# Cross attentions of a two-layer decoder: scores, mask and maximum in pairs of units, and the end of the layer normalisation on GpSimd

## What is computed

```python
def _layernorm(x, axis=-1, eps=1e-05):
    m = jnp.mean(x, axis=axis, keepdims=True)
    v = jnp.var(x, axis=axis, keepdims=True)
    return (x - m) / jnp.sqrt(v + eps)

def _L0_xattn_ref(query, key, value, mask, Wq, bq, Wk, bk, Wv, bv, Wo, bo):
    ...
    scores = jnp.einsum('bhqd,bhkd->bhqk', Q, K) / np.sqrt(D_K)
    m = mask[:, None, :, :]
    scores = jnp.where(m == 0, NEG, scores)
    attn = jax.nn.softmax(scores, axis=-1)
    x = jnp.einsum('bhqk,bhkd->bhqd', attn, V)
    x = x.transpose(0, 2, 1, 3).reshape(b, -1, D_MODEL)
    return x @ Wo.T + bo

x = _layernorm(x + _L0_attn_ref(...))
x = _layernorm(x + _L0_xattn_ref(x, ctx_1024, ctx_1024, mask_BxSxS2_ik0, ...))
x = _layernorm(x + _L0_ffn_ref(...))
x = _layernorm(x + _L1_attn_ref(...))
x = _layernorm(x + _L1_xattn_ref(x, ctx_1024, ctx_1024, mask_Bx1xSxS2_ff0, ...))
x = _layernorm(x + _L1_ffn_ref(...))
```

## Time and profile before

| | |
|---|---|
| median of three runs | 1294.27 us (1292.2 to 1297.17) |
| the profiled execution, its own time | 1291.09 us |
| its span, first to last instruction | 1289.3 us |
| mean granted TensorE clock | 0.924 of full speed |
| busy: PE, DVE, ACT, POOL | 84%, 75%, 55%, 30% of the span |
| first cross attention, first to last score turned | 436.8 to 580.8 us |
| second cross attention, the same | 1055.7 to 1197.2 us |

### The profile page before, as it was taken

The page is one execution under the profiler, slowest core; times in us unless marked ns, Lnnn a source line. Parts: engine busy times, 40 slices in busy tenths (PEclk is TensorE's granted clock), DMA queues, the critical chain, the costliest instruction groups (busy, mean ns, idle before and its releaser), DMA issues. The chain is left out here.

```text
span 1289.3 us, 30260 instructions
## 1 busy us (share of the span) xinstructions
PE 1087.8 (84%) x10763; PEld 881.4 (68%) x10763; DVE 961.6 (75%) x2254; ACT 704.9 (55%) x1459; POOL 388.9 (30%) x538
## 2 busy tenths in 40 slices
PE   4899989999987699986269999389999569999696
PEld 3578878778776577774257777378787447777485
DVE  7587877878875488884938883569998538888497
ACT  2454444444443355552637775368788525655484
POOL 5122222222220355551130000423331225555232
PEclk9899999999999799995559999699999879999799
DMA  6000000100000500005245431300000000000011
GB/s 257 5 10 2 10 12 2 71 3 2 2 2 2 187 23 22 11 9 227 107 135 172 171 108 49 120 17 26 24 9 9 0 24 23 11 21 9 34 50 50
DMA packets 34072, 65.35 MB, mean 51 GB/s; under 512 B 7590, under 2 KB 23334, under 8 KB 30886
## 3 DMA queue, kind: packets, MB, share of 16 engines
q1 hardware_dynamic: 32422, 59.62, 13.2%
q0 software_dynamic: 1536, 4.20, 1.0%
HBM read 43.03 MB, written 12.39 MB: 43 GB/s over the span
## 5 line engine op out<-in xcount | busy, mean ns | idle before, releaser
L953 POOL TENSOR_TENSOR ca_z<-ca_z,ca_top 128x308 f32<-128x308 f32 x128 | 92.7, 724 | 129.8 <-DVE ca_top L1082 129.5
L389 ACT ACTIVATE wa_probs<-wa_scores,wa_minus_top 128x192 f32<-128x192 f32 x256 | 83.3, 437 | 80.6 <-DVE wa_minus_top L477 80.6
L1025 ACT ACTIVATE ca_pth<-ca_turned 77x512 f16<-77x512 f32 x128 | 75.9, 593 | 59.0 <-PE ca_turned L1209 58.4
L348 POOL TENSOR_TENSOR wa_q<-wa_by_cos,wa_by_sin 128x256 f32<-128x256 f32 x32 | 23.4, 732 | 266.3 <-DVE wa_by_sin L472 266.3
L1209 PE MATMUL ca_turned<-ident,ca_probs 128*77 128x128 f32 x512 | 84.1, 287 | 20.6 <-ACT ca_probs L1017 19.5
L400 ACT ACTIVATE wa_pth<-wa_turned 128x384 f16<-128x384 f32 x128 | 58.4, 506 | 73.5 <-PE wa_turned L696 73.5
L1200 PE MATMUL ca_scores<-ca_km,ca_q 128*128 128x308 f32 x256 | 89.6, 433 | 6.0 <-ACT ca_q L998 5.7
L1087 DVE SCALAR_TENSOR_TENSOR ca_ptl<-ca_turned,ca_pth 77x512 f16<-77x512 f32 x128 | 86.7, 677 | 2.6 <-ACT ca_pth L1025 2.6
L1017 ACT ACTIVATE ca_probs<-ca_z 128x308 f32<-128x308 f32 x128 | 58.2, 455 | 44.8 <-POOL ca_z L953 43.8
L621 PE MATMUL wa_scores<-wa_xh,wa_wh 128*128 128x256 f16 x256 | 70.5, 275 | 11.7 <-DVE wa_wl L456 9.7
L477 DVE TENSOR_REDUCE wa_minus_top<-wa_scores 128x2 f32<-128x384 f32 x128 | 62.3, 549 | 21.1 <-PE wa_scores L684 18.9
(11 more groups left out here) (332 smaller groups left out, 3677.0 us busy)
## 6 DMA issues: line engine op xcount, KB each, us to landing
ex_stage<-in_ew SPq DMA_DIRECT2D x16, 1024.0 KB, 7.0
slots<-slots_zeros SPq DMA_DIRECT2D x10, 512.0 KB, 5.3
ca_xs<-tokens SPq DMA_DIRECT2D x16, 256.0 KB, 2.3
ex_xe<-slots SPq DMA_DIRECT2D x11, 320.0 KB, 3.3
slots<-ex_y SPq DMA_DIRECT2D x9, 320.0 KB
wa_x_stage<-in_xt SPq DMA_DIRECT2D x8, 256.0 KB, 3.0
tokens<-in_x SPq DMA_DIRECT2D x1, 2048.0 KB, 14.8
ca_w<-in_xw SPq DMA_DIRECT2D x2, 1024.0 KB, 5.6
```

The source lines that it names most:

```text
L389: ins = act.activation(probs[2 * (u % 2) + t][:, h, t * WINDOW:t * WINDOW + SPAN], s_bank[i][:, t * SPAN:(t + 1) * SPAN], ACT.Exp, bias=mi ...
L953: pool.tensor_tensor(z[k][:], z[k][:], top[:, k].unsqueeze(2).broadcast_to((P, UH, CTX)), ALU.subtract).then_inc(shift, 1)
L1025: act.activation(pth[k][0:CTX], t_bank[k][0:CTX], ACT.Copy, scale=PSCALE).then_inc(probs_high, 1)
```

## The change

- The scores of two units are made together (`score_pair`): two products of 64 rows of contraction each, rows 0 to 63 for the first four heads of a group of eight and rows 64 to 127 for the other four, into two PSUM banks that now are one tensor. They stand at the end of slots 1, 3, 5 and 7 (units c + 3 and c + 4; for the next batch in slots 5 and 7).
- `mask_scores` and `take_maximum` take eight heads (616 columns) in the even slots, right behind each other and ahead of the low half. `subtract` and `power` still take four heads. `z` and `top` hold two pairs.
- The ring moves `tokens` from slot 4 to slot 2 and `query` from slot 5 to slot 4.
- The last step of the normalisation goes from VectorE to GpSimd: after the root, one subtraction of the mean (`y`) and one multiplication. For tile 0 of the last batch that stands in slot 0 behind the subtraction of unit 2, for tile 1 in slot 4 behind that of unit 6; for the last batch at the end.
- `value_low` moves from slot 2 to slot 3, the low half (`probs_rest`) behind `normalise`.

```diff
@@ CA
         [("key", 0)],
         [("value", 0)],
-        [("heads", 1)],
+        [("heads", 1), ("tokens", 0)],
         [("mix", 1)],
-        [("tokens", 0)],
         [("query", 0)],
+        [],
         [("heads", 0)],
         [("mix", 0)],
@@ tiles
-        z = [sb(f"z{k}", [P, UH, CTX]) for k in range(2)]
-        top = sb("top", [P, 2, UH])
+        z = [sb(f"z{k}", [P, 2 * UH, CTX]) for k in range(2)]
+        top = sb("top", [P, 2, 2 * UH])
+        y = sb("y", [P, TPB, DIM])
-        s_bank = [ctx.enter_context(nc.psum_tensor(f"{tag}_scores{k}", [P, 512], F32)) for k in range(2)]
+        s_banks = ctx.enter_context(nc.psum_tensor(f"{tag}_scores", [P, 2 * UH, P], F32))
@@ GpSimd
             def subtract(b, c):
-                pool.wait_ge(maxed, b * UNITS + c + 1)
+                pool.wait_ge(maxed, b * PAIRS + c // 2 + 1)
...
+            def layer_norm(b, t):
+
+                norm.root(pool, b, t)
+                pool.wait_ge(norm.rstd_ready, b * TPB + t + 1)
+                pool.tensor_tensor(y[:, t], norm.res[:, t], norm.mv[:, t, 0:1].broadcast_to((P, DIM)),
+                                   ALU.subtract).then_inc(norm.ln_done, 1)
+                pool.wait_ge(norm.ln_done, b * TPB + t + 1)
+                pool.tensor_tensor(at(X, b * TPB + t), y[:, t], norm.rstd[:, t].broadcast_to((P, DIM)), ALU.mult)
...
+                    if c == 0 and before:
+                        layer_norm(b - 1, 0)
                     if c == 4 and before:
-                        norm.root(pool, b - 1, 1)
+                        layer_norm(b - 1, 1)
                     if c in (5, 6):
                         add_bias(b, par, c - 5)
-                    if c == 7:
-                        norm.root(pool, b, 0)
@@ VectorE
-                dve.wait_ge(scores, b * UNITS + c + 1)
-                if not (first(b) and c < 2):
-                    dve.wait_ge(exped, b * UNITS + c - 1)
+                dve.wait_ge(scores, b * PAIRS + c // 2 + 1)
+                if not (first(b) and c < 4):
+                    dve.wait_ge(exped, b * UNITS + c - 2)
...
+                if not first(b):
+                    dve.wait_ge(norm.ln_done, (b - 1) * TPB + t + 1)
                 dve.tensor_tensor(norm.res[:, t], shared[bank][:, 0:DIM], xb[:, t], ALU.add).then_inc(free[bank], 1)
...
-                    if two_on:
+                    if two_on and c % 2 == 0:
                         mask_scores(*two_on)
-                    probs_rest(b, c)
-                    if two_on:
                         take_maximum(*two_on)
                     if c == 5:
                         normalise(b, 0)
                     if c == 1 and before:
                         normalise(b - 1, 1)
+                    probs_rest(b, c)
...
-                    if c == 0 and before:
-                        norm.apply(dve, b - 1, 0, at(X, (b - 1) * TPB))
-                    if c == 5 and before:
-                        norm.apply(dve, b - 1, 1, at(X, (b - 1) * TPB + 1))
-                    if c == 2 and after:
+                    if c == 3 and after:
                         value_low(b + 1, 1 - par)
@@ TensorE
+            def score_pair(b, c, par):
...
+                if not (first(b) and c == 0):
+                    pe.wait_ge(masked, b * PAIRS + c // 2)
+                for k in range(2):
+                    rows = slice(HALF * k, HALF * (k + 1))
+                    ins = pe.matmul(s_banks[:, UH * k:UH * (k + 1), 0:CTX], q[par][rows, g, t * P:(t + 1) * P],
+                                    km[par][rows, g, UH * k:UH * (k + 1)], start=True, stop=True)
+                ins.then_inc(scores, 1)
...
                     turn_probs(b, c)
-                    if c < UNITS - 2:
-                        score(b, c + 2, par)
-                    elif after:
-                        score(b + 1, c + 2 - UNITS, 1 - par)
...
+                    if c in (1, 3):
+                        score_pair(b, c + 3, par)
+                    if c in (5, 7) and after:
+                        score_pair(b + 1, c - 5, 1 - par)
```

More of the change, by code:

```diff
@@ L774 @@
 UH = 4
+HALF = UH * CD
 UNITS = TPB * CH // UH
+PAIRS = UNITS // 2
 MASKED = -4.0e9
@@ L950, in subtract @@
             def subtract(b, c):
[L951 to L953 removed]
+                pool.wait_ge(maxed, b * PAIRS + c // 2 + 1)
+                k = c // 2 % 2
+                heads = slice(UH * (c % 2), UH * (c % 2 + 1))
+                pool.tensor_tensor(z[k][:, heads], z[k][:, heads], top[:, k, heads].unsqueeze(2).broadcast_to((P, UH, CTX)),
                                    ALU.subtract).then_inc(shift, 1)
@@ L982, in _ @@
             both(batch)(pool)
-            norm.root(pool, BATCH - 1, 1)
+            layer_norm(BATCH - 1, 0)
+            layer_norm(BATCH - 1, 1)
         @block.scalar
@@ L1016, in power @@
                     act.wait_ge(probs_t, b * UNITS + c - 1)
-                act.activation(probs[k][:], z[k][:], ACT.Exp, scale=1.0 if additive else CD ** -0.5).then_inc(exped, 1)
+                act.activation(probs[k][:], z[c // 2 % 2][:, UH * k:UH * (k + 1)], ACT.Exp, scale=1.0 if additive else CD ** -0.5).then_inc(exped, 1)
             def batch(b, par, before=True, after=True):
@@ L1065, in mask_scores @@
             def mask_scores(b, c):
-                k = c % 2
-                dve.wait_ge(scores, b * UNITS + c + 1)
-                if not (first(b) and c < 2):
-                    dve.wait_ge(exped, b * UNITS + c - 1)
-                s = s_bank[k][:, 0:UH * CTX].rearrange("p (h k) -> p h k", h=UH)
-                m = at(mask if additive else limit, b * TPB + c // (UNITS // TPB)).unsqueeze(1).broadcast_to((P, UH, CTX))
+                k = c // 2 % 2
+                dve.wait_ge(scores, b * PAIRS + c // 2 + 1)
+                if not (first(b) and c < 4):
+                    dve.wait_ge(exped, b * UNITS + c - 2)
+                s = s_banks[:, :, 0:CTX]
+                m = at(mask if additive else limit, b * TPB + c // (UNITS // TPB)).unsqueeze(1).broadcast_to((P, 2 * UH, CTX))
                 if additive:
@@ L1141, in _ @@
                 dve.wait_ge(limits, 2)
-            for c in range(2):
-                mask_scores(0, c)
-                take_maximum(0, c)
+            mask_scores(0, 0)
+            take_maximum(0, 0)
             both(batch)(dve)
-            norm.apply(dve, BATCH - 1, 0, at(X, (BATCH - 1) * TPB))
             normalise(BATCH - 1, 1)
@@ L1190, in step @@
                 ins.then_inc(full[bank], 1)
-            def score(b, c, par):
+            def score_pair(b, c, par):
                 t, part = divmod(c, UNITS // TPB)
-                g, h = part // 2, UH * (part % 2)
+                g = part // 2
                 if c == 0:
@@ L1197, in score @@
                     pe.wait_ge(key_masked, (b + 1) * KT_)
-                if not (first(b) and c < 2):
-                    pe.wait_ge(masked, b * UNITS + c - 1)
-                pe.matmul(s_bank[c % 2][:, 0:UH * CTX], q[par][:, g, t * P:(t + 1) * P],
-                          km[par][:, g, h:h + UH].rearrange("p h k -> p (h k)"), start=True, stop=True).then_inc(scores, 1)
+                if not (first(b) and c == 0):
[5 more added lines that the diff above has]
+                ins.then_inc(scores, 1)
             def turn_probs(b, c):
@@ L1244, in _ @@
                 step(0, 0, kind, i, bank, uses)
-            score(0, 0, 0)
-            score(0, 1, 0)
+            score_pair(0, 0, 0)
+            score_pair(0, 2, 0)
             both(batch)(pe)
```

7 lines of the change are left out of this document (2 added, 5 removed).

## The result

The changed kernel takes 1300.79 us, the median of 20 executions (1294.68 to 1301.82), where the kernel before takes 1295.00 in the same runs (20 executions, 1290.3 to 1299.67): a ratio of 1.0035, 95% interval 1.0022 to 1.0048. By the prediction's bound of 0.5% that is no change, though the interval leaves out 1: the kernel is about 4.5 us slower. Two later groups of runs gave 1.0035 (1.0017 to 1.0053) and 1.0027 (1.0007 to 1.0046). The profiled execution took 1301.13 us, with a span of 1299.4 and a mean granted clock of 0.910 (before 1291.09, 1289.3 and 0.924).

A forecast was written before the change was run, and what follows sets the result against it. A chain through several queues was taken to bound the kernel: 18.47 against 18.35 us a batch, +1.4 over twelve batches, +0.6 at stage ends, +2.0 on 1291.1, and 3.2 to the median, gives 1296.3; range 1282 to 1307.

The forecast's parts named there:

- The loop: Chain through all queues from one pair's mask to the next, twice a batch; claimed to set the batch at 18.47 us.
- The half with the value's low half: Second of the loop's two passes, with value's low half in slot 3 and turned tokens on ScalarE: 7.47 + L.
- The back edge: Longer way from residual to mask, 1.90 against 1.29, every second batch: adds 0.61 there, counted as 0.30 a batch.
- L: GpSimd's root, mean subtraction and multiplication between a pair's two subtractions: 1.94 us, bounds 1.75 and 2.26.
- The rival of 0.77 each: Slower rival: GpSimd's two new instructions cost as with two full operands, L = 2.26, batch 19.11, 1304 us; chance 0.22.
- The pair: TensorE's 64-row score products side by side: 0.82 us instead of 1.04, bounds 0.52 and 1.34.
- that rival: Slower rival: the two 64-row products don't overlap, pair 1.34, batch 18.9, total 1306 us; chance 0.06.
- One sign: Among what would show the forecast right in the new profile: VectorE without a wait for scores.
- The pair's 0.22 buys nothing: TensorE's own work, 16.7 us a batch, is shorter than the loop's 18.47, so the cheaper score pair saves no time.
- The faster rival, loop not closed: Masks come earlier or L is under 1.4, so TensorE sets the batch: 17.2 us, total 1282; chance 0.25.
- +0.3 a stage, within 1 either way: Net cost at the ends of each cross attention: first turn, batch 0, batch 7 and the very end together.
- a credit of 1.2: Batch 0 of each cross attention has no normalisation in its way, so some 1.2 us shorter.

The follow-up runs named there:

- slot 6 filled: Changed kernel with six further transposes on TensorE ahead of the two in slot 6, run twice: 1299.57 us (ratio 1.0044) and 1298.62 (1.0023).
- whole rows: Changed kernel with the last two products of each score pair over all 128 rows instead of 64 each: 1294.53 us, ratio 1.0004.
- normalisation behind both: Changed kernel with the GpSimd normalisation one slot later, behind the pair's second subtraction (slots 1 and 5), mask_keys moved behind it: 1285.01 us, ratio 0.9936.
- third group: The changed kernel itself, unaltered, measured again in a later group of runs: 1299.77 us, ratio 1.0027.
- filled after pairs: Changed kernel, 64-row pairs kept, with three further transposes on TensorE behind each score pair, ahead of the wait for exponentials: 1299.66 us, ratio 1.0031.
- pairs alone: Changed kernel with the normalisation back on VectorE (slots 0 and 5) and the roots back in GpSimd's slots 4 and 7: 1291.84 us, ratio 0.9973.
- normalisation alone: Kernel before with only the normalisation moved to GpSimd, single score products, masks and maxima kept: 1306.98 us, ratio 1.0097.

## Why the prediction was right, and where not

The forecast was 1296.3, no change; measured were 1300.79 and a ratio of 1.0035. The class and the range hold, in part by luck: against the kernel before the forecast was +2.0 us and +4.5 came, of 6.5 that still count as no change, and the range of 1282 to 1307 was wide enough to hold the rivals too. The mechanism holds in nearly every term of the loop. What failed is the sum outside it, above all the clock, which the prediction did not name.

- **The loop.** Predicted 18.47 a batch, measured 18.37 where no batch of 1 to 6 had a low clock (110.2 for six; the kernel with slot 6 filled, whose quiet batches are those of the changed one), before 18.35. The half with the value's low half: predicted 7.47 + 1.94 = 9.41, measured 9.31 (1117.32 to 1126.63). The other: 8.76 predicted, 8.83 measured (1126.63 to the mask at 1135.46). The back edge: 0.30 predicted on average, 0.24 measured (18.62, the mean of every second batch, against 18.13, by two). Ten latencies from quiet places added up to within 0.1.
- **L.** Predicted 1.94, measured 2.00. The two new instructions take 0.614 each, where I took 0.61 by the repeated operand; the other 0.06 is the gap between them, 0.19 where I had 0.13. The rival of 0.77 each (1304) falls. The Trainium skill (GPSIMD Engine Reference, section 3.1 Elementwise) gives about 2.6 cycles an element for a `tensor_tensor`, and its clock of 1.2 GHz makes that an estimate of 0.55 us for 256 elements before any fixed cost. The 0.614 here is in line with it; for 616 elements the same figure gives 1.33, and the trace has 1.22.
- **The pair.** Predicted 0.82, measured 0.72 from the first product to the next turn, with all four records in one row of 0.79, where four products of 308 columns one after the other take 1.12 (whole rows): they overlap, so that rival falls too. It is 0.2 over the 0.52 side by side, the loss that the earlier trace rows show. The rule of the Trainium skill (TensorEngine Tiling (Array Packing), section Tiling Modes) that a change of mode drains TensorE is in line with this 0.2, though no run tells a drain from another loss. A gap of 0.12 stands ahead of the pair, so the slots came out as forecast: 2.47 (2.47), 2.53 (2.5), 1.69 (1.7), and slots 2 and 6 at 2.15 and 2.22 (2.1). One sign did not hold: VectorE still waits for scores, if little (1.5 us from 1080 to 1180, 9.2 before).
- **"The pair's 0.22 buys nothing".** Right, and shown by whole rows: same batches, to 0.02.
- **The faster rival, loop not closed.** It named 17.2 a batch for a loop set by TensorE. The normalisation behind both subtractions opened the loop, and a quiet batch took 17.23. My statement of the price was right for the order that was given, and I did not ask what order would avoid it.
- **The step that failed: "+0.3 a stage, within 1 either way", and all durations at full clock.** The trace of before showed the clock at 1.00 over the whole of the earlier trace rows, and I summed as if it would stay. With work taken off TensorE and the batch no shorter, TensorE idled 1.05 us in a row in each slot 6; the clock then fell, one or more times in a stage (+1.0 net each), and at the starts and in batch 7. Against the profile before, the parts other than batches 1 to 6 of the changed kernel (third group) cost +1.2 and +4.7; predicted were 0.3 each. Of that, +0.9 and +0.7 are the start (predicted, +0.9). Batch 0, where I had a credit of 1.2, took 1.4 less in the first stage, at low clock in both kernels, and 1.4 more in the second, where only the changed kernel was at low clock. Batch 7 cost +0.9, and +1.9 with a spell, where 0.6 were predicted. The end, where I had set off +1.0 against -1.0, cost +0.8.

How much of the 4 us goes with the clock can be read from more than the profiles, since every execution of the three later groups, and of the changed kernel, has its span and its mean granted clock recorded. Over the 81 executions of the kernel before, the span falls by 0.78 us for each 0.001 of mean clock (a straight line; correlation -0.94). The last column is how far a kernel's mean span lies above that line, so it compares kernels at the same clock.

| kernel | executions | mean clock | mean span | above the line |
|---|---|---|---|---|
| before | 81 | 0.9210 | 1293.7 | 0 |
| changed | 44 | 0.9170 | 1297.7 | +0.9 |
| whole rows | 10 | 0.9240 | 1293.6 | +2.3 |
| slot 6 filled | 20 | 0.9171 | 1297.1 | +0.4 |
| filled after pairs | 12 | 0.9211 | 1297.2 | +3.6 |
| pairs alone | 12 | 0.9142 | 1289.5 | -9.5 |
| normalisation alone | 6 | 0.9240 | 1304.0 | +12.6 |
| normalisation behind both | 6 | 0.9197 | 1282.2 | -12.6 |

The changed kernel is 4.0 us longer in the mean; 3.1 go with its lower clock, and 0.9 are left, where the prediction had 2.0. In the profiles the difference lies in the two stages: 59 to 64 us at low clock there, against 27 of the kernel before and 37 with whole rows, while the rest of the program has no more of it than before (157 to 169 against 169). Whole rows bring the clock back (7 thousandths, 5.5 us by the line) and cost 1.4 of it. The fill behind the pairs brings back 4 thousandths (3.2) and costs 2.7; the fill of slot 6 doesn't bring it back, since batches 0 and 7 stay low. The line shows what goes together, not what causes what. That TensorE's idle time lowers the clock inside the loop is supported by the three runs with fills and by whole rows, none of which has a low spell in batches 1 to 6; it isn't the whole of it, as the spell behind 0.52 of idle and the holes of 0.85 without one show.

What stays open is why the kernel before, which has a busy time of nothing in the 1.5 us ahead of its first turn, was at full clock there in its second cross attention and at 0.50 in its first:

```profile
1054.17:1055.67 1.50, 0.00 (x1) 0.00 (x1) 1.03 (x3) 0.46 (x1) 1.05 (x2) 1.00 0.00 0
435.33:436.83 1.50, 0.00 (x1) 0.00 (x1) 1.03 (x3) 0.46 (x1) 1.06 (x2) 0.50 1.09 385
```

Idle time just before is thus not all that decides there.

## What to carry to other kernels

Before a step is handed to an engine with free time, ask what stands behind it in that engine's queue: the same two instructions, with their root, cost 0.9 us a batch between two subtractions and, in the loop, nothing behind them. Where a loop through several queues sets the pace, making one engine's work cheaper doesn't shorten it; a run with the dearer form tells at once whether the saving reached the time. And look at the clock in the stretches that stay the same: TensorE with holes may lose more in its next products than the saving was.

## What the runs showed of the hardware

- In the changed kernel the granted clock fell from 1.00 to 0.50 for 3.4 us at a time in one to three of the six middle batches of a stage. All eight falls in its three profiles began within the hole of 1 us that every batch has in slot 6, or at most 0.12 us behind it; the other 28 such holes had no fall. Each fall cost 1.0 to 1.1 us net. With TensorE's hole filled, or its products made longer, there was none in the middle batches.
- 0.4 us more of products per score pair made the whole program 5 us faster (1294.53 against 1299.75).
- On GpSimd an instruction of 256 elements with one operand repeated takes 0.614 us, one of the same size with two full ones 0.725, or 0.769 in the kernel before (groups of the changed kernel: busy us, mean ns of one, idle before):

```profile
L965 POOL TENSOR_TENSOR ca_xb<-ca_xs,ca_rows 128x256 f32<-128x256 f32 x32 | 23.1, 725 | 0.0
...
L971 POOL TENSOR_TENSOR ca_y<-ca_res,ca_mv 128x256 f32<-128x256 f32 x32 | 19.6, 614 | 2.5
```
